# Linear attention and a butterfly feed-forward layer on one core: zeros for TensorE in the first pauses, a new order in the first and last slots, and all layer norms applied by VectorE

## The chip, the core and the metric

The kernel runs on one core of a Trainium2 chip. A core has a matrix engine (TensorE, PE in the rows; its weight loads are PEld), VectorE (DVE), ScalarE (ACT), GpSimd (POOL) and SyncE (SP), which here only issues DMAs. Each engine takes its own instructions in order and waits on semaphores for the others. The metric is the device time of one execution in microseconds (us), lower is better.

## The reference

One post-norm block on `x` of 4 x 1024 tokens with 128 features, in fp32:

```python
q, k, v = split(x @ W_qkv)                       # 16 heads of 64
q, k = relu(q @ W_f + b_f), relu(k @ W_f + b_f)  # per head
kv = einsum('bhnd,bhne->bhde', k, v)
out = einsum('bhnd,bhde->bhne', q, kv)
out = out / (einsum('bhnd,bhd->bhn', q, k.sum(2))[..., None] + 1e-6)
x1 = layernorm(x + out @ W_out + b_out)
h = butterfly(x1 @ W_exp + b_exp, up_weights)    # 512 features, 9 stages
h = butterfly(gelu(h + up_bias), down_weights)
y = layernorm(x1 + h @ W_con + b_con + down_bias)
```

## The kernel before

Weights are folded once on the chip: W_f into the key and query weights, the two butterflies into W_exp (by GpSimd, `up_step`) and W_con (by VectorE, nine steps `down_term`, `down_term`, `down_sum`, semaphore `s_dn`, three counts a step). Large fp32 products are split into a high and a low fp32r part, and three products make one (`split`, L671).

The tokens are 32 tiles of 128, and 8 chunks of 512. All engines walk through the same 43 slots (`SLOTS`), and each engine's code is a loop over the slots with its steps written out in order. Until slot 27 a slot holds: keys of a tile in two halves (`project_k`, taken by VectorE's `k_max`), the sum of keys times x (`add_kx`), two query steps (`project_q`, taken by ScalarE), two attention steps (`add_attn`, which need `qn`, its high part by ScalarE and its low part by VectorE's `qn_lo`), and, in some slots, up and down products of the feed-forward. The row names: `ring` is a ring of three PSUM banks that keys, queries, normalisers and up products share; `desk`, `spare_ps` and `attn_ps` are single banks; `kx_ps` holds the keys times x; `late` is the copied attention output; `hid` the hidden layer.

A use of the ring waits until the use three before it has been emptied. In a slot with a normaliser (every fourth) the order is key half 0, normaliser, query, key half 1, query, up product, so key half 1 waits for `k_max` of key half 0.

VectorE's order in a slot is: `k_max` of half 0, two `normalise_q`, then what the slot has of `reciprocal`, `m_lo`, `xT_lo`, `x1T_lo`, then `qn_lo`, `k_max` of half 1, `kx_end`, the residual sum with the statistics of a layer norm (`add_x` for norm 0, which makes x1, or `residual` for norm 1, which makes y), `qn_lo`. GpSimd raises the variance to the power -1/2 (`rstd_of`, L599). The norm is applied by ScalarE in the next slot (`layer_norm_apply`, L1134) before slot `APPLY_END` = 35, and by VectorE in the same slot, behind its last `qn_lo`, from there on (`layer_norm_end`, L1399).

The reciprocal of the normaliser goes to DRAM in four DMAs and comes back spread over partitions in eight (`spread`), on SP's queue, between the loads of butterfly coefficients, each of which waits for a step of the butterfly:

```python
load_down(5)
load_down(6)
spread(0)
load_down(7)
```

The first attention step (`add_attn(0)`, in slot 11) waits for `s_dn` at 3 * `PS_LAST` = 21, since steps 1 to `PS_LAST` - 1 of the butterfly keep their second term in `attn_ps`.

Of the kernel before, what the change touches and what calls it, by code (L numbers as in the profile page):

```python
# [5 lines left out]
def postln_linear_attention_butterfly_ffn_kernel(  # L6
# [102 lines left out]
    MAPS_SLOT = {}  # L109
    for b in range(BATCH):  # L110
        MAPS_SLOT[TILES * b + ATTN_AT - 2] = (b, 0)
        MAPS_SLOT[TILES * b + ATTN_AT - (0 if b else 1)] = (b, 1)
    XT_SLOT = {2: (1, 0), 3: (1, 1), 8: (2, 0), 11: (2, 1)}
    for b in range(3, BATCH):
        XT_SLOT[TILES * b - 6] = (b, 0)
        XT_SLOT[TILES * b - 5] = (b, 1)
    ATTN_LAST = [ATTN_AT + (PAIRS // 2) * (n + 1) - 1 for n in range(ALLCH)]
    ATT_T_SLOT = {ATTN_LAST[n] + 1: n for n in range(LAST)}
    X1T_SLOT = {ATTN_LAST[n] + 2: n for n in range(LAST)}
    UPS = {}  # L120
    DOWN_SLOT = {}
    Y_SLOT = {}
# [61 lines left out]
    for s in range(SLOTS):  # L184
        order = []
        if s in ATT_T_SLOT:
            order.append(("attn", ATT_T_SLOT[s]))
        if s in KXT_SLOT:
            order.append(("kxT", *KXT_SLOT[s]))
        if s in MAPS_SLOT:  # L190
            order.append(("maps", *MAPS_SLOT[s]))
        if s == BIAS_T_SLOT:
            order.append(("bias",))
        if s in XT_SLOT and s <= max(DOWN_STEP_SLOT):
            order.append(("x", *XT_SLOT[s]))
        if s == FIRST:
            order.append(("vo", 3))
        if s in X1T_SLOT:
            order.append(("x1", X1T_SLOT[s]))
        for use in order:  # L200
            desk_of[use] = len(desk_of)
# [19 lines left out]
    with ctx:  # L221
        def sb(name, shape, dt=fp32):
            return ctx.enter_context(nc.sbuf_tensor(name, shape, dt))
# [213 lines left out]
        def _(sp):  # L437
# [57 lines left out]
            column(bout_col[:, :], b_out)  # L495
            for i in range(HT):
                column(bup_raw[:, i:i + 1], up_bias[i * 128:(i + 1) * 128])
            def spread(n):

                sp.wait_ge(s_r, n + 1)  # L500
                for j in range(4):
                    sp.dma_start(recip_rows[n, :, j * QT:(j + 1) * QT], recip[32 * j:32 * j + 2 * PAIRS, :])\
                        .then_inc(s_rst, 16)
                sp.wait_ge(s_rst, 64 * (n + 1))
# [24 lines left out]
            load_down(3)  # L529
            load_down(4)  # L530
            load_down(5)
            load_down(6)
            spread(0)
            load_down(7)
            load_down(8)
            for n in range(1, LAST + 4):
                if n >= 4:

                    store_out(n - 4)
                if n < ALLCH:  # L540
                    spread(n)
# [12 lines left out]
        def _(pool):  # L554
# [75 lines left out]
            for s in range(SLOTS):  # L630
                if s == WEIGHTS_SLOT:
                    pool.wait_ge(s_wuh, 1)
                    g.tensor_tensor(wup_l[:, :], y_up[:, :], wup_h[:, :].bitcast(fp32), ALU.subtract).then_inc(s_wul, 1)
                if s == WEIGHTS_SLOT:
                    pool.wait_ge(s_rows, 48)
                    g.tensor_tensor(bdn_row, bdn_row, bcon_row, ALU.add).then_inc(s_brow, 1)
                if s in ATT_T_SLOT:
                    rstd_of(0, ATT_T_SLOT[s])
                if s in Y_SLOT:
                    rstd_of(1, Y_SLOT[s])  # L640
                if s in X1T_SLOT:
                    with_bias(X1T_SLOT[s], slice(0, QUADS), X1T_SLOT[s] + 1)
# [23 lines left out]
        def _(pe):  # L666
# [228 lines left out]
            def transpose_first_x(part):  # L895
# [2 lines left out]
                    last = t_.transpose(kx_ps[part][:, i * 128:(i + 1) * 128], xs[0][:, 2 * part + i, 0:C], ident[:, :])  # L898
                last.then_inc(s_xp, 1)

            pe.wait_ge(s_const, 2)
            transpose_first_x(0)
            pe.wait_ge(s_wk[0], 16)
            transpose_weights(PAIRS, 2, ring[0]).then_inc(s_wT, 1)
            transpose_first_x(1)
            pe.wait_ge(s_wf, 32)
            pe.wait_ge(s_wTd, 1)
            fold_wf(PAIRS, 2, attn_ps)

            for s in range(SLOTS):  # L910
                for kt in k_tiles(s)[:1]:
# [130 lines left out]
                down_group(LAST - 1, i, spare_ps[:, i * 128:(i + 1) * 128]).then_inc(s_dgrp, 1)  # L1042


            transpose_x1_half(0)
            take_down(LAST - 1)
            down_before_last(0)
            transpose_x1_half(1)
            down_before_last(1)
            up_half(0)  # L1050
            down_before_last(2)
            down_before_last(3)
# [9 lines left out]
        def _(act):  # L1062
# [89 lines left out]

            act.wait_ge(s_xp, 1)
            hi(xT_h[:, 0, 0:256], kx_ps[0][:, 0:256], s_x01h)
            act.wait_ge(s_xp, 2)
            hi(xT_h[:, 0, 256:CH], kx_ps[1][:, 0:256], s_xTh)
            act.wait_ge(s_fold, 1)
            hi(wk_h[:, 0:256], attn_ps[:, 0:256], s_wh)
            act.wait_ge(s_bf, 16)
            a_.activation(bf_minus[:, :], bf_row[:, :], ACT.Copy, scale=-1.0).then_inc(s_bfm, 1)  # L1160

            for s in range(SLOTS):
# [98 lines left out]
        def _(dve):  # L1261
# [177 lines left out]
            lo(xT_l[:, 0, 0:256], kx_ps[0][:, 0:256], xT_h[:, 0, 0:256], s_x01l)  # L1439
            dve.wait_ge(s_xTh, 1)  # L1440
            lo(xT_l[:, 0, 256:CH], kx_ps[1][:, 0:256], xT_h[:, 0, 256:CH], s_xTl)
            dve.wait_ge(s_wh, 1)
            lo(wk_l[:, 0:256], attn_ps[:, 0:256], wk_h[:, 0:256], s_wl)

            def w_lo(n, dst, high):
                dve.wait_ge(s_wh, n)
# [2 lines left out]
            for s in range(SLOTS):  # L1449
# [23 lines left out]
                for kt in k_tiles(s)[:1]:  # L1473
                    k_max(kt, 1)
                if s == 0:
                    w_lo(2, wk_l[:, 256:CH], wk_h[:, 256:CH])
                if s == 1:
                    w_lo(3, wk_l[:, CH:2 * CH], wk_h[:, CH:2 * CH])
                if s == 2:
# [2 lines left out]
                for kt in k_tiles(s)[1:]:  # L1482
                    k_max(kt, 0)
                if s == 0:
                    v.reduce_sum(x_part[:, 0, 1:2], desk[:, :], axis=mybir.AxisListType.X).then_inc(s_dtaken, 1)
                    v.reduce_sum(x_part[:, 0, 0:1], kx_both[:, :].rearrange("p (a n) -> p a n", a=2)[:, :, 0:256],
                                 axis=mybir.AxisListType.XY).then_inc(s_xpart, 1)
                if s == 1:
                    w_lo(4, wq_l[:, 0:CH], wq_h[:, 0:CH])
                for kt in k_tiles(s)[1:]:  # L1490
                    k_max(kt, 1)
                if s == 3:
                    down_term(0, 1)
                if s in KXT_SLOT:
# [55 lines left out]
                layer_norm_half(0, g, attn_ps[:, g * HALF:(g + 1) * HALF], xs[(BATCH - 1) % XBUF][:, at:at + 2, 0:C],  # L1550
                                last_x1[:, tiles, :], (s_x1sum, g + 1))
            layer_norm_half_end(0, 0, last_x1, s_x1)
            layer_norm_end(1, LAST - 2, y[:, (LAST - 2) % 2, :, :], s_yo)
            layer_norm_half_end(0, 1, last_x1, s_x1)
            for g in range(2):
                tok = slice(g * HALF, (g + 1) * HALF)
                use = ("x1", LAST, g)
                dve.wait_ge(s_x1h, LAST + 1 + g)
                lo(x1T_l[:, tok], half_bank(use)[:, 0:HALF], x1T_h[:, tok], half_taken(use)[0])
# [35 lines left out]
```

## Time and profile before

| | |
|---|---|
| median of 3 runs | 324.87 us (323.04 to 325.10) |
| profiled execution | 323.96 us, its rows span 322.1 us |
| TensorE busy | 302.8 us, 94% |
| VectorE busy | 218.7 us, 68% |
| ScalarE busy | 142.6 us, 44% |
| GpSimd busy | 96.0 us, 30% |
| mean granted clock of TensorE | 0.996 |

The profiled execution lies 1.86 us above its span and 0.91 us below the median. Times in rows are counted from the start of the span.

### The profile page before, as it was taken

What the parts mean: (1) busy time and instruction counts of PE and PEld (TensorE: products, weight loads), DVE (VectorE), ACT (ScalarE), POOL (GpSimd) and SP (SyncE); (2) the same over time, 40 slices, a digit from 0 to 9 for tenths busy, and PEclk for the clock granted to TensorE, in tenths of its full rate; (3) what the DMA queues carried; (4) which work ended last, traced back from release to release, by engine and by line L of the source; (5) the groups of instructions that cost most, each with busy time, mean ns of one, the idle gap of its engine ahead of it and who ended that gap; (6) DMA issues with size and microseconds to landing.
All of it is one profiled execution on the core that took longest, in us unless ns stands there. A gap on an engine that the chain in (4) does not pass through costs nothing.

```text
span 322.1 us, 6555 instructions
## 1 busy us (share of the span) xinstructions
PE 302.8 (94%) x2521; PEld 268.2 (83%) x2521; DVE 218.7 (68%) x492; ACT 142.6 (44%) x267; POOL 96.0 (30%) x105
## 2 busy tenths in 40 slices
PE   4799999999699999999999999999999799999893
PEld 2799999988598898988899989998887587759793
DVE  4535568887898978658763794269548953768844
ACT  3223133324333454554562467256657846340452
POOL 3048998992000002400210121003203402513413
PEclk9999999999999999999999999999999999999998
DMA  5993493224922900640074005600190182462001
GB/s 133 288 335 106 126 263 136 113 86 140 240 85 75 211 5 7 163 101 0 4 171 94 2 36 121 146 0 35 38 225 5 40 200 62 117 159 55 1 35 65
DMA packets 23046, 34.02 MB, mean 106 GB/s; under 512 B 4040, under 2 KB 11112, under 8 KB 23016
## 3 DMA queue, kind: packets, MB, share of 16 engines
q1 hardware_dynamic: 22712, 33.54, 39.8%
q8 instruction: 20, 0.33, 0.4%
q10 hardware_dynamic: 304, 0.07, 0.1%
q14 instruction: 10, 0.08, 0.1%
HBM read 31.24 MB, written 2.36 MB: 104 GB/s over the span
## 4 chain that ended last, share of the span: by engine, by line
PE 79%; DVE 8%; issue 5%; DMA 3%; ACT 2%; SPq 1%; POOL 1%; POOLq 0%; DVEq 0%; ACTq 0%
PE ring L671 30%; PE kx_ps L770 16%; PE attn_ps L671 9%; PE spare_ps L871 8%; PE ring L788 4%; PE desk L680 3%; PE desk L802 2%; DMA recips<-recip_rows 1%; PE attn_ps L709 1%; DVE qn L1375 1%; PE attn_ps L822 1%; DVE stats L1384 1%; DMA xs<-in_L_attn_x_dram 1%; DMA recip_rows<-recip 1%; PE attn_ps L828 1%
## 5 line engine op out<-in xcount | busy, mean ns | idle before, releaser
L1327 DVE TENSOR_TENSOR k<-ring,bf_minus 128x512 f32<-128x512 f32 x64 | 43.9, 687 | 46.6 <-PE ring L671 46.5
L599 POOL TENSOR_TENSOR rstd<-var_eps,minus_half 128x4 f32<-128x4 f32 x14 | 19.3, 1380 | 164.8 <-DVE var_eps L1390 164.8
L1079 ACT ACTIVATE q<-ring,bf_col 128x512 f32<-128x512 f32 x64 | 43.7, 684 | 53.1 <-PE ring L671 52.9
L770 PE MATMUL kx_ps<-xs,k 128*128 128x129 f32 x512 | 62.4, 275 | 1.6 <-issue 1.6
L770 PEld LDWEIGHTS kx_ps<-xs,k 128*128 128x128 f32 x512 | 61.1, 191 | 3.4 <-issue 1.8
L1375 DVE TENSOR_TENSOR qn<-q,recips 128x512 f32<-128x512 f32 x64 | 43.3, 716 | 3.3 <-DMA recips<-recip_rows 3.3
L1071 ACT ACTIVATE qn_h<-qn 128x512 fp32r<-128x512 f32 x48 | 29.6, 627 | 26.8 <-DVE qn L1375 26.8
L671 PE MATMUL ring<-wk_h,xT_h 128*128 128x256 f32 x128 | 39.3, 307 | 1.0 <-DVE wk_l L1265 1.0
L1265 DVE TENSOR_TENSOR qn_l<-qn,qn_h 128x512 fp32r<-128x512 f32 x48 | 33.8, 712 | 7.7 <-ACT qn_h L1071 7.0
L671 PE MATMUL ring<-wk_l,xT_h 128*128 128x256 f32 x128 | 36.4, 284 | 0.0
L671 PE MATMUL ring<-wk_h,xT_l 128*128 128x256 f32 x128 | 36.4, 284 | 0.0
L582 POOL TENSOR_TENSOR y<-hid,y_up 128x512 f32<-128x512 f32 x18 | 27.6, 1557 | 18.5 <-DMA hid<-in_L_ffn_up_weights_dram 17.6
L1143 ACT ACTIVATE hid<-ring,bup_col 128x512 f32<-128x512 f32 x28 | 19.2, 687 | 22.9 <-PE ring L671 22.7
L671 PE MATMUL ring<-xT_h,wq_h 128*128 128x512 f32 x64 | 27.7, 434 | 0.0
L671 PEld LDWEIGHTS ring<-wk_h,xT_h 128*128 128x128 f32 x128 | 24.8, 193 | 3.3 <-issue 1.6
L871 PEld LDWEIGHTS spare_ps<-wdn,hid 128*128 128x128 f32 x224 | 25.9, 192 | 1.0 <-issue 0.8
L871 PE MATMUL spare_ps<-wdn,hid 128*128 128x128 f32 x224 | 26.7, 276 | 0.0
L671 PEld LDWEIGHTS ring<-wk_l,xT_h 128*128 128x128 f32 x128 | 24.9, 194 | 1.6
L671 PE MATMUL ring<-xT_h,wq_l 128*128 128x512 f32 x64 | 25.3, 395 | 0.0
L671 PE MATMUL ring<-xT_l,wq_h 128*128 128x512 f32 x64 | 25.2, 393 | 0.0
L671 PEld LDWEIGHTS ring<-wk_h,xT_l 128*128 128x128 f32 x128 | 24.7, 193 | 0.0
L671 PE MATMUL attn_ps<-qn_h,m_h 128*128 128x512 f32 x48 | 19.6, 407 | 3.1 <-issue 2.6
(158 smaller groups left out, 526.4 us busy)
## 6 DMA issues: line engine op xcount, KB each, us to landing
recips<-recip_rows SPq DMA_DIRECT2D x64, 256.0 KB, 5.5
hid<-in_L_ffn_up_weights_dram SPq DMA_DIRECT2D x9, 512.0 KB, 4.7
x<-_L_ffn_down_weights_dram SPq DMA_DIRECT2D x9, 512.0 KB, 3.9
xs<-in_L_attn_x_dram SPq DMA_DIRECT2D x7, 256.0 KB, 5.5
out_dram<-y SPq DMA_DIRECT2D x7, 256.0 KB, 2.1
q<-in_L_attn_W_qkv_dram SPq DMA_DIRECT2D x2, 512.0 KB, 5.5
q<-in_L_attn_W_out_dram SPq DMA_DIRECT2D x2, 256.0 KB, 7.7
recip_rows<-recip SPq DMA_DIRECT2D x32, 8.0 KB, 1.4
```

Of the source, the lines that this page charges most:

```text
L582: g.tensor_tensor(term_up[f].rearrange("p (hi j lo) -> p hi j lo", j=2, lo=lo), w[:, :, :, :, f], yv[:, :, f:f + 1, :].to_broadcast([128, ...
L599: g.tensor_tensor(rstd[i][:, :], var_eps[i][:, :], minus_half[:, :].to_broadcast([128, QUADS]), ALU.pow).then_inc(s_rs[i], 1)
L671: last = t_.matmul(dst, lhsT, rhs, start=start and n == 0, stop=stop and n == len(pairs) - 1)
L770: last = t_.matmul(kx_ps[g % 2][:, j * C1:(j + 1) * C1], k[kt % KRING][:, col:col + 128], xs[b % XBUF][:, QUADS * c + 2 * half + i, :], st ...
L788: last = t_.matmul(dst[32 * j:32 * j + 32, 0:QT], ksum_cols[:, p, :], q[:, (PAIRS * n + p) % QRING, j * QT:(j + 1) * QT], start=p == 0, st ...
L871: last = t_.matmul(dst, hid[:, j, i * 128:(i + 1) * 128], wdn[:, j, :], start=j == 0, stop=j == HT - 1)
L1071: a_.activation(dst, src, ACT.Copy).then_inc(done, 1)
L1079: a_.activation(q[:, i % QRING, :], bank(("q", i))[:, :], ACT.Relu, bias=bf_col[:, :])\
L1143: a_.activation(hid[:, i, :], bank(("up", f))[:, :], ACT.Gelu, bias=bup_col[:, i:i + 1])\
L1265: v.tensor_tensor(dst, src, high.bitcast(fp32), ALU.subtract).then_inc(done, 1)
L1327: v.tensor_tensor(k[kt % KRING][:, half * CH:(half + 1) * CH].rearrange("p (h d) -> p h d", d=D), bank(("k", kt, half))[:, :].rearrange("p ...
L1375: v.tensor_tensor(qn[:, a % NRING, :], q[:, a % QRING, :], recips[:, a % PAIRS // RC, a % RC, :], ALU.mult).then_inc(s_qn, 1)
```

## The change

Seven edits that stand apart:

- VectorE clears a tile `zeros` first of all, and TensorE multiplies it by itself 20 times before its first work, 6 times before the first fold of W_f, and 4 times before the first keys. The results go to `desk` and are not read.
- The first fold is put ahead of the transposes of the second half of the first x, with its followers on ScalarE and VectorE. In slot 0 VectorE makes `x_part` of `kx_ps`, for which `add_kx(0)` waits, earlier.
- `PS_LAST` is 6.
- The store of the reciprocal is split from `spread`, and for chunk 0 it stands ahead of `load_down(6)`.
- The second half of `head_maps` stands one slot earlier for all batches but the first.
- `APPLY_END` is 0: nine layer norms, five of x1 and four of y, leave ScalarE; the `mean_minus` and `offset` that ScalarE's form needs go with them. The transposes of x1 of chunk 4 go from the end of slot 32 to slot 33, behind its two query steps.
- At the end, TensorE's first down group of chunk 6 stands ahead of the transposes of the last x1, and VectorE applies both halves of the last x1 before the norm of y of chunk 5.

```diff
-        MAPS_SLOT[TILES * b + ATTN_AT - (0 if b else 1)] = (b, 1)
+        MAPS_SLOT[TILES * b + ATTN_AT - 1] = (b, 1)
...
-    X1T_SLOT = {ATTN_LAST[n] + 2: n for n in range(LAST)}
+    X1T_HEAD = {ATTN_LAST[4] + 3: 4}
+    X1T_SLOT = {ATTN_LAST[n] + 2: n for n in range(LAST) if n not in X1T_HEAD.values()}
...
-    APPLY_END = 35
+    APPLY_END = 0
...
-    PS_LAST = 7
+    PS_LAST = 6
...
             load_down(5)
+            store_recip(0)
             load_down(6)
             spread(0)
...
+            def multiply_zeros(n):
+                for _ in range(n):
+                    t_.matmul(desk[:, 0:128], zeros[:, :], zeros[:, :], start=True, stop=True)
+
+            pe.wait_ge(s_zeros, 1)
+            multiply_zeros(20)
             pe.wait_ge(s_const, 2)
             transpose_first_x(0)
             pe.wait_ge(s_wk[0], 16)
             transpose_weights(PAIRS, 2, ring[0]).then_inc(s_wT, 1)
-            transpose_first_x(1)
+            multiply_zeros(6)
             pe.wait_ge(s_wf, 32)
             pe.wait_ge(s_wTd, 1)
             fold_wf(PAIRS, 2, attn_ps)
+            transpose_first_x(1)
+            multiply_zeros(4)
...
-            transpose_x1_half(0)
             take_down(LAST - 1)
             down_before_last(0)
+            transpose_x1_half(0)
+            down_before_last(1)
             transpose_x1_half(1)
-            down_before_last(1)
...
                 if s == 0:
-                    w_lo(2, wk_l[:, 256:CH], wk_h[:, 256:CH])
+                    v.reduce_sum(x_part[:, 0, 0:1], kx_both[:, :].rearrange("p (a n) -> p a n", a=2)[:, :, 0:256],
+                                 axis=mybir.AxisListType.XY).then_inc(s_xpart, 1)
...
             layer_norm_half_end(0, 0, last_x1, s_x1)
-            layer_norm_end(1, LAST - 2, y[:, (LAST - 2) % 2, :, :], s_yo)
             layer_norm_half_end(0, 1, last_x1, s_x1)
             for g in range(2):
+                if g:
+                    layer_norm_end(1, LAST - 2, y[:, (LAST - 2) % 2, :, :], s_yo)
```

TensorE's first instructions, before (`kx_ps<-ident,xs` are transposes of x, `ring<-ident,q` of key weights, `attn_ps<-wf_diag,q` is the fold, `ring<-wk_h,xT_h` the first key product):

```order
L898 MATMUL kx_ps<-ident,xs 128x128 x2
L702 MATMUL ring<-ident,q 128x128 x2
L898 MATMUL kx_ps<-ident,xs 128x128 x2
L709 MATMUL attn_ps<-wf_diag,q 128x128 x2
L671 MATMUL ring<-wk_h,xT_h 128x256
```

And in the changed kernel, at the same place of TensorE's program:

```order
L916 MATMUL desk<-zeros 128x128 x20
L910 MATMUL kx_ps<-ident,xs 128x128 x2
L714 MATMUL ring<-ident,q 128x128 x2
L916 MATMUL desk<-zeros 128x128 x6
L721 MATMUL attn_ps<-wf_diag,q 128x128 x2
L910 MATMUL kx_ps<-ident,xs 128x128 x2
L916 MATMUL desk<-zeros 128x128 x4
L683 MATMUL ring<-wk_h,xT_h 128x256
```

The fold has moved ahead of the second transposes of x, and thirty products of zeros stand in between.

VectorE from the residual of slot 22 to the attention operands of slot 23, before (`y<-spare_ps,y` is `residual`, `k<-ring` is `k_max`, `qn_l` is `qn_lo`, `qn<-q,recips` is `normalise_q`):

```order
L1419 TENSOR_TENSOR y<-spare_ps,y 128x512
L1384 BN_STATS stats<-y 128x6 x4
L1386 MEMSET scratch 128x1
L1388 BN_AGGR mean_var<-stats 128x2 x4
L1390 TENSOR_SCALAR var_eps<-mean_var 128x4
L1393 TENSOR_SCALAR mean_minus<-mean_var 128x4
L1265 TENSOR_TENSOR qn_l<-qn,qn_h 128x512
L1327 TENSOR_TENSOR k<-ring,bf_minus 128x512
L1375 TENSOR_TENSOR qn<-q,recips 128x512 x2
L1265 TENSOR_TENSOR qn_l<-qn,qn_h 128x512
```

The same stretch of VectorE in the changed kernel:

```order
L1444 TENSOR_TENSOR y<-spare_ps,y 128x512
L1409 BN_STATS stats<-y 128x6 x4
L1411 MEMSET scratch 128x1
L1413 BN_AGGR mean_var<-stats 128x2 x4
L1415 TENSOR_SCALAR var_eps<-mean_var 128x4
L1290 TENSOR_TENSOR qn_l<-qn,qn_h 128x512
L1424 TENSOR_SCALAR y<-y,mean_var,rstd 128x128 x4
L1352 TENSOR_TENSOR k<-ring,bf_minus 128x512
L1400 TENSOR_TENSOR qn<-q,recips 128x512 x2
L1290 TENSOR_TENSOR qn_l<-qn,qn_h 128x512
```

Four instructions that apply the norm now stand between `qn_lo` and the next slot's `k_max`, and `mean_minus` is gone.

TensorE from the last up product of slot 32 to the first attention product of slot 33, before (`ring<-x1T...` is an up product, `desk<-ident,x` transposes x1 of chunk 4, `ring<-xT...,wq` are queries):

```order
L671 MATMUL ring<-x1T_h,wup_l 128x512
L680 MATMUL desk<-ident,x 128x128 x4
L671 MATMUL ring<-xT_h,wq_h 128x512
L671 MATMUL ring<-xT_l,wq_h 128x512
L671 MATMUL ring<-xT_h,wq_l 128x512
```

And in the changed kernel:

```order
L683 MATMUL ring<-xT_l,wq_h 128x512
L683 MATMUL ring<-xT_h,wq_l 128x512
L692 MATMUL desk<-ident,x 128x128 x4
L683 MATMUL attn_ps<-qn_h,m_h 128x512
L683 MATMUL attn_ps<-qn_l,m_h 128x512
```

The transposes have moved behind both query steps and stand directly ahead of the attention steps of slot 33.

## Rows read from the trace of the kernel before

**Rows 1.** Busy time per stretch: length, PE, PEld, DVE, ACT, POOL, clock, DMA share, GB/s.

```profile
16.00:66.00 50.00, 50.00 (x401) 48.48 (x402) 32.45 (x43) 14.91 (x28) 42.11 (x33) 1.00 0.57 178
89.00:246.00 157.00, 156.83 (x1330) 139.54 (x1329) 109.44 (x242) 81.54 (x152) 19.10 (x18) 1.00 0.33 77
```

**Rows 2.** Timeline of the start: start, busy time, engine, line, [idle before <-releaser].

```profile
1.23 1.76 DVE L1435 MEMSET q<- 128x2048 f32 x1 [1.23 <-PEq L1584]
...
3.27 0.66 PE L898 MATMUL kx_ps<-ident,xs 128*128 128x128 f32 x2 [3.27 <-POOL head_mask L569]
...
7.53 0.55 PE L671 MATMUL ring<-wk_h,xT_h 128*128 128x256 f32 x1 [1.02 <-DVE wk_l L1265]
...
8.31 0.41 PE L671 MATMUL ring<-wk_h,xT_h 128*128 128x256 f32 x1
...
8.53 0.41 PE L671 MATMUL ring<-wk_l,xT_h 128*128 128x256 f32 x1
...
12.27 0.28 PE L671 MATMUL ring<-wk_h,xT_h 128*128 128x256 f32 x1
...
12.39 0.28 PE L671 MATMUL ring<-wk_l,xT_h 128*128 128x256 f32 x1
...
15.22 0.68 DVE L1486 TENSOR_REDUCE x_part<-kx_ps 128x1 f32<-128x512 f32 x1
...
16.00 2.02 PE L770 MATMUL kx_ps<-xs,k 128*128 128x129 f32 x16 [1.63 <-issue]
```

**Rows 3.** Timeline of slots 8 to 11, DVE, SP's queue and PE.

```profile
68.80 0.95 DVE L1359 RECIPROCAL recip<-recip 128x128 f32<-128x128 f32 x1 [1.48 <-ACT recip L1117]
...
72.65 1.82 SPq L502 DMA_DIRECT2D recip_rows<-recip  x4
...
81.89 1.29 DVE L1375 TENSOR_TENSOR qn<-q,recips 128x512 f32<-128x512 f32 x2 [1.66 <-DMA recips<-recip_rows]
...
83.84 1.09 PE L802 MATMUL desk<-vo,kx 128*64 128x128 f32 x16 [0.44 <-DVE m_l L1265]
...
87.67 0.70 DVE L1294 TENSOR_TENSOR spare_ps<-late,attn_ps 128x512 f32<-128x512 f32 x1
...
88.47 0.47 PE L671 MATMUL attn_ps<-qn_h,m_h 128*128 128x512 f32 x1 [2.63 <-issue]
```

**Rows 4.** Timeline, slots 22 to 24, and VectorE's apply in a later slot.

```profile
183.57 1.46 POOL L599 TENSOR_TENSOR rstd<-var_eps,minus_half 128x4 f32<-128x4 f32 x1 [19.55 <-DVE var_eps L1390]
...
184.07 0.68 DVE L1327 TENSOR_TENSOR k<-ring,bf_minus 128x512 f32<-128x512 f32 x1
...
190.05 0.69 DVE L1327 TENSOR_TENSOR k<-ring,bf_minus 128x512 f32<-128x512 f32 x1
...
193.12 0.28 PE L671 MATMUL ring<-wk_h,xT_h 128*128 128x256 f32 x1
...
277.65 1.12 DVE L1399 TENSOR_SCALAR x<-x,mean_var,rstd 128x128 f32<-128x128 f32 x4 [0.90 <-POOL rstd L599]
```

**Rows 5.** Timeline, slots 31 to 33.

```profile
248.11 1.18 POOL L647 TENSOR_TENSOR xs<-xs,rows 128x512 f32<-128x512 f32 x1
...
248.19 1.65 DVE L1265 TENSOR_TENSOR qn_l<-qn,qn_h 128x512 fp32r<-128x512 f32 x1
...
251.95 0.69 DVE L1265 TENSOR_TENSOR qn_l<-qn,qn_h 128x512 fp32r<-128x512 f32 x1
...
252.78 0.47 PE L671 MATMUL attn_ps<-qn_h,m_h 128*128 128x512 f32 x1
...
256.19 0.63 PE L680 MATMUL desk<-ident,x 128*128 128x128 f32 x4 [1.76 <-ACT x L1134]
...
258.05 0.40 PE L671 MATMUL attn_ps<-qn_h,m_h 128*128 128x512 f32 x1
```

**Rows 6.** Timeline of PE, slot 35 and the end.

```profile
274.68 1.09 PE L802 MATMUL desk<-vo,kx 128*64 128x128 f32 x16 [0.47 <-DVE x L1408]
...
305.64 0.41 PE L1026 MATMUL desk<-ident,x 128*128 128x128 f32 x2 [1.08 <-DVE x L1539]
```

More of the change, by code:

```diff
@@ L187, in postln_linear_attention_butterfly_ffn_kernel @@
             order.append(("attn", ATT_T_SLOT[s]))
+        if s in X1T_HEAD:
+            order.append(("x1", X1T_HEAD[s]))
         if s in KXT_SLOT:
@@ L253, in postln_linear_attention_butterfly_ffn_kernel @@
         warm = sb("warm", [128, 1])
+        zeros = sb("zeros", [128, 128], fp32r)
         minus_half = sb("minus_half", [128, 1])
@@ L344, in postln_linear_attention_butterfly_ffn_kernel @@
         s_zero = sem("zeroed")
+        s_zeros = sem("zeros_for_tensor_made")
         s_wfz = sem("wf_zeroed")
@@ L497, in _, with store_recip @@
                 column(bup_raw[:, i:i + 1], up_bias[i * 128:(i + 1) * 128])
-            def spread(n):
+            def store_recip(n):
                 sp.wait_ge(s_r, n + 1)
@@ L503, in spread @@
                         .then_inc(s_rst, 16)
+            def spread(n):
                 sp.wait_ge(s_rst, 64 * (n + 1))
@@ L540, in _ @@
                 if n < ALLCH:
+                    store_recip(n)
                     spread(n)
@@ L640, in _ @@
                     rstd_of(1, Y_SLOT[s])
-                if s in X1T_SLOT:
-                    with_bias(X1T_SLOT[s], slice(0, QUADS), X1T_SLOT[s] + 1)
+                for at in (X1T_SLOT, X1T_HEAD):
+                    if s in at:
+                        with_bias(at[s], slice(0, QUADS), at[s] + 1)
                 if s == NO_KEYS + 2:
@@ L920, in _ @@
                         project_q(i)
+                if s in X1T_HEAD:
+                    transpose_x1(X1T_HEAD[s])
                 for a in adds(s)[:1]:
@@ L1154, in _ @@
             hi(xT_h[:, 0, 0:256], kx_ps[0][:, 0:256], s_x01h)
+            act.wait_ge(s_fold, 1)
+            hi(wk_h[:, 0:256], attn_ps[:, 0:256], s_wh)
             act.wait_ge(s_xp, 2)
             hi(xT_h[:, 0, 256:CH], kx_ps[1][:, 0:256], s_xTh)
-            act.wait_ge(s_fold, 1)
-            hi(wk_h[:, 0:256], attn_ps[:, 0:256], s_wh)
             act.wait_ge(s_bf, 16)
@@ L1169, in _ @@
                         q_relu(i)
+                if s in X1T_HEAD:
+                    x1T_hi(X1T_HEAD[s])
                 if s in LATE_NORM_SLOT:
@@ L1433, in x1T_lo @@
                 lo(x1T_l[:, :], desk[:, :], x1T_h[:, :], s_dtaken)
+            v.memset(zeros[:, :].bitcast(fp32), 0.0).then_inc(s_zeros, 1)
             v.memset(wout_diag, 0.0).then_inc(s_zero, 1)
@@ L1439, in _ @@
             lo(xT_l[:, 0, 0:256], kx_ps[0][:, 0:256], xT_h[:, 0, 0:256], s_x01l)
+            dve.wait_ge(s_wh, 1)
+            lo(wk_l[:, 0:256], attn_ps[:, 0:256], wk_h[:, 0:256], s_wl)
             dve.wait_ge(s_xTh, 1)
             lo(xT_l[:, 0, 256:CH], kx_ps[1][:, 0:256], xT_h[:, 0, 256:CH], s_xTl)
-            dve.wait_ge(s_wh, 1)
-            lo(wk_l[:, 0:256], attn_ps[:, 0:256], wk_h[:, 0:256], s_wl)
             def w_lo(n, dst, high):
@@ L1468, in _ @@
                     x1T_lo(X1T_SLOT[s - 1])
+                if s in X1T_HEAD:
+                    x1T_lo(X1T_HEAD[s])
                 if s in DOWN_STEP_SLOT:
@@ L1484, in _ @@
                 if s == 0:
-                    v.reduce_sum(x_part[:, 0, 1:2], desk[:, :], axis=mybir.AxisListType.X).then_inc(s_dtaken, 1)
-                    v.reduce_sum(x_part[:, 0, 0:1], kx_both[:, :].rearrange("p (a n) -> p a n", a=2)[:, :, 0:256],
-                                 axis=mybir.AxisListType.XY).then_inc(s_xpart, 1)
+                    w_lo(2, wk_l[:, 256:CH], wk_h[:, 256:CH])
                 if s == 1:
@@ L1491, in _ @@
                     k_max(kt, 1)
+                if s == 0:
+                    v.reduce_sum(x_part[:, 0, 1:2], desk[:, :], axis=mybir.AxisListType.X).then_inc(s_dtaken, 1)
                 if s == 3:
```

## Prediction

> **What bounds the kernel now.** I read the busy time by stretch first, since the share over the whole span mixes stages. From 16 to 66 us and from 89 to 246 us TensorE is busy for 50.00 of 50.00 and 156.83 of 157.00 us at a granted clock of 1.00, while VectorE works for 32.45 and 109.44 us of them [rows 1]. In these two stretches nothing but less work for TensorE can help, and no edit takes real work from it. So a gain must come from where TensorE waits. I looked for those places in the timeline of TensorE: the start, up to 16.00 us [rows 2]; slots 8 to 11 [rows 3]; the end of slot 32, where it waits 1.76 us [rows 5]; slot 35, 0.47 us, and the last transposes of x1, 1.08 us [rows 6]. For the moves on VectorE I asked the reverse: which TensorE instruction needs the result that now comes later, and how long before it that result was there [rows 4, 5]. What is won at the start isn't eaten by a later wait that I could find, because TensorE has no idle time between 16 and 66 us on which a load could have been about to arrive late.
>
> **The start.** TensorE starts with two transposes at 3.27 us, after a wait for GpSimd's constants. Its first key product starts at 7.53, after 1.02 us of waiting for the low part of the folded key weights. Key products then follow each other 0.22 us apart (8.31 to 8.53), but 0.12 apart from 12.27 on (to 12.39), and `add_kx(0)` starts at 16.00 after 1.63 us of idle time, with `x_part` ready at 15.22 + 0.68 = 15.90 [rows 2]. The spacing falls by a factor of two, as it would between TensorE's levels of 1.2 and 2.4 GHz. The slower pace ends some 4.5 us after TensorE became continuously busy at 7.53.
>
> The zeros can begin when VectorE has cleared their tile: it starts its first MEMSET at 1.23 us [rows 2], and one of 128 columns instead of 2048 takes about 1.76 / 16 = 0.11, so at about 1.4. No row shows an fp32r product of 128 columns. By columns it is half of one of 256, 0.11 us at the slow pace; at worst it costs what an fp32 product of 129 columns does, 2.02 / 16 = 0.126 at the fast pace [rows 2], so 0.25 at the slow. Twenty take 2.2 to 5.0 us and end between 3.6 and 6.4, where the transposes stood at 3.27. I take 0.11, since the rows of the same type are nearer. The fold then stands ahead of the second transposes, and the weights' low part ahead of VectorE's second x; the keys start at about 6.85 instead of 7.53. If TensorE is at the fast pace by 7.5, as 4.5 us from about 1.4 and the gaps between let me expect, its work from 7.53 to 14.37 (16.00 less 1.63) takes 6.84 - 2.3 = 4.5 us instead, since the slow 4.6 us up to 12.1 halve; that ends at 11.4, and 0.3 later for a slow beginning. `x_part` of `kx_ps` moves ahead of a weight split and two `k_max`, so that the 1.63 us goes, but for the 0.3 that VectorE still needs. `add_kx(0)` then starts at 12.0: **-4.0 us**. If the pace doesn't rise sooner, only the fold (0.7) and the idle time (1.3) are won, -2.0; the other end is -4.5.
>
> The Trainium skill, "TensorE: Matmul & The Clock Gate", has a clock for TensorE that rises when it has been kept busy and falls back in pauses, which agrees with the halved spacing in rows 2. By it products of zeros count as work, and the start comes out at the -4.0; no run here shows that yet.
>
> **Slots 8 to 11.** The first attention product waits 2.63 us until 88.47, behind a sum of VectorE that begins at 87.67 and takes 0.70 [rows 3]. That is step 6 of the butterfly. With `PS_LAST` at 6 the count is reached by step 5, a slot earlier, and the 2.63 goes. The reciprocal is ready at 68.80 + 0.95 = 69.75, but its store is issued only at 72.65, behind a coefficient load that waits for the butterfly. VectorE later waits 1.66 us for the spread copy, ahead of the `qn` at 81.89, and the maps' low part keeps TensorE waiting 0.44 at 83.84 [rows 3]. With the store 2.9 us earlier the 1.66 should go, and with it most of the 0.44. I count 2.63 + 0.44 = 3.07 and **-3.1**. What is late next is VectorE itself: if it isn't done with `qn_l` when the count is there, only about half is won, -1.5. If its 1.66 also shortens a stall of the keys behind it, it is -3.4. `load_down(6)` now stands behind the store, but the wait for step 5 on the same queue ends later than the reciprocal, so it pays nothing.
>
> **The maps.** In batches 1 to 3 half of `head_maps` comes a slot sooner. In slots 18 and 26 it meets `desk` just after the transposes of the keys' sum, which VectorE has to empty; by my reading of the same pair of steps in slot 35 (0.47 us of waiting [rows 6]) I take 0.25 for each, **+0.5**, bounds 0 and 0.94. For the third batch, slot 35's own 0.47 and a restart of 0.1 go: **-0.6**.
>
> **Layer norms on VectorE.** Each of the nine costs VectorE its wait for GpSimd's power and four scalings. In the slot that does this already it waits 0.90 us and works 1.12 [rows 4], so about 2.0 us each, 18 in all. ScalarE is rid of as much, but TensorE never waits for ScalarE except for the 1.76 us of rows 5. VectorE is idle for 47.6 us between 89 and 246 (157.00 - 109.44 [rows 1]), which is the cover of most. It fails where two norms lie in succession and VectorE has no gaps: slots 22 and 23, whose neighbours have a normaliser. There the power of slot 22 is ready at 183.57 + 1.46 = 185.03, whereas `k_max` started at 184.07. In slot 24 `k_max` of half 0 ends at 190.05 + 0.69 = 190.74, and TensorE's key half 1, which needs its bank, starts at 193.12: cover 2.38 [rows 4]. Two norms bring 4.1 and 190.74 becomes 194.8, so TensorE waits **+1.7**, bounds 0 and 2.5. The pairs in slots 15/16, 19/20 and 26/27 have larger gaps on VectorE around them, and I cost them at nothing; without that cover each would cost the same 1.7.
>
> In slots 30 to 33 VectorE has no slack: its `qn_l` of 251.95 ends at 252.64, and the attention product that needs it starts at 252.78 [rows 5]. Here the norm of y delays the next attention step by up to 2.0, and the norm of x1 the one behind it, while the transposes of chunk 4 no longer wait 1.76 for ScalarE. I have the attention product of 258.05 at 258.4 to 259.4, so **+0.9**; the bounds are -1.9 (all hidden and the 1.76 won) and +1.9. One `qn_l` in this stretch takes 1.65 us instead of 0.69, while GpSimd adds at 248.11 for 1.18 [rows 5].
>
> The Trainium skill, "GPSIMD Engine Reference", says that GpSimd and VectorE share access to SBUF; the 1.65 beside 0.69 agrees with that. By it an apply that meets GpSimd's work is stretched by up to the same 0.96, and the term would be +1.9 rather than +0.9.
>
> **The end.** The 1.08 us before the last transposes of x1 [rows 6] is filled by a down group that stood behind them, and the second half of x1 no longer waits for y's norm: **-1.1**, bounds 0 and -1.5.
>
> **The sum.** -4.0 - 3.1 + 0.5 - 0.6 + 1.7 + 0.9 - 1.1 = -5.7. The profiled execution took 323.96, which gives 318.3; from the median of 324.87, 0.91 higher, it is 319.2. The runs lie between 323.04 and 325.10, with the profiled one in the middle, so I lean to it: **318.5 us**. About 1%, 3.2 us, is what a measurement of this kernel can tell from no change.
>
> **The rivals.**
> - All norms hidden. For it: VectorE's 47.6 idle us. Against it: the cover of 2.38 in rows 4. Without +1.7 and +0.9, and with part of the 1.76, the time is 314 to 316; by both ends of all gains 313.5. Chance 0.2.
> - The zeros don't bring the fast pace sooner, or the pauses between them lose it again. For it: three waits remain between the groups of zeros. Start -2.0, so 320.5. Chance 0.15.
> - VectorE is late at slots 8 to 11. For it: the wait for the copy is VectorE's own, and it works without a gap behind it. -1.5 instead of -3.1, so 320.1. Chance 0.1.
> - Slow zeros: 0.25 a product puts the first transposes 3.1 us later and the keys at about 11 us; the fast pace then gives back what this takes, and the start is worth 0. 322.5. Chance 0.06.
> - Slower than before: the norms reach TensorE in most slots, because VectorE's wait for GpSimd puts every later `k_max`, `qn` and `qn_l` of the slot behind it. The gains without norms are 8.3 us. At 2.0 a norm this turns the sign from five uncovered ones on; all nine give 324 - 8.3 + 18 = 334. For it: the order itself, in which nothing passes the waiting apply. Against it: TensorE's lead of 2.38. Chance 0.04.
>
> The forecast itself has 0.45. The range 313.5 to 322 leaves out the slower case and the outer ends of two terms at once. Faster by over 1% (below 321.6): the forecast, the first three rivals nearly whole: 0.85. Within 1%: slow zeros and the outer parts of two others, 0.11. Slower 0.04.
>
> **What the changed profile would show.** Right: key products 0.12 apart from 7.5 us on; `add_kx(0)` near 12; the first attention product with no 2.63 ahead of it and `store_recip` at 70; nine waits of VectorE for `rstd` of about 0.9, and TensorE idle in slot 24 for some 1.7; no 1.76 at the transposes of chunk 4; the last transposes without 1.08. Wrong: a TensorE gap that grows behind `k_max` in several slots, a first transpose after 4 us, or a load of weights that TensorE now waits for before 66 us, since everything there comes 4 us sooner.

## The result and the profile after

The changed kernel is slower: 329.45 us against 324.52 in the median, a ratio of 1.0142 with a 95% interval of 1.0091 to 1.0193. The prediction said 318.5 and, with a chance of 0.85, faster. The profiled execution took 330.15 us and spans 328.4, 6.3 more than before. The first line of its page and the shares of its chain of waits by engine:

```profile
PE 310.5 (95%) x2551; PEld 274.8 (84%) x2551; DVE 228.5 (70%) x520; ACT 129.3 (39%) x231; POOL 93.6 (29%) x96
...
PE 78%; DVE 9%; issue 6%; POOL 3%; ACT 2%; POOLq 0%; DVEq 0%; ACTq 0%
```

TensorE is busier by 7.7 us though its real work is the same: 6.6 us lie between the starts of the zeros and of what follows them, and in slot 27 products ran at half pace. GpSimd is now on the chain with 3%; those are the powers for which VectorE's norms wait.

Where the 6.3 us arise is best read by putting the starts of the same TensorE instructions side by side. The last column is what a stretch added or took.

| TensorE instruction | before | after | later by | stretch |
|---|---|---|---|---|
| first `add_kx(0)` | 16.00 | 15.70 | -0.30 | start -0.3 |
| first attention product, slot 11 | 88.47 | 84.85 | -3.62 | slots 8 to 11 -3.3 |
| last attention step of slot 18 | 141.71 | 138.00 | -3.71 | -0.1 |
| first attention step of slot 20 | 157.91 | 155.84 | -2.07 | slots 18, 19 +1.6 |
| last of slot 24 | 193.83 | 193.44 | -0.39 | slots 22 to 24 +1.7 |
| last of slot 26 | 212.43 | 212.04 | -0.39 | 0 |
| first of slot 28 | 228.56 | 233.43 | +4.87 | slots 26, 27 +5.3 |
| last of slot 33 | 258.74 | 265.15 | +6.41 | slots 29 to 33 +1.5 |
| end of the span | 322.1 | 328.4 | +6.3 | -0.1 |

Two stretches are far from the forecast: the start and slots 26 and 27. The start first, in the timeline of the changed kernel, against [rows 2]:

```profile
1.05 4.53 PE L916 MATMUL desk<-zeros 128*128 128x128 f32 x20 [1.05 <-DVE zeros L1460]
5.38 0.65 PE L910 MATMUL kx_ps<-ident,xs 128*128 128x128 f32 x2
...
9.61 0.55 PE L683 MATMUL ring<-wk_h,xT_h 128*128 128x256 f32 x1
...
10.39 0.41 PE L683 MATMUL ring<-wk_h,xT_h 128*128 128x256 f32 x1
10.60 0.41 PE L683 MATMUL ring<-wk_l,xT_h 128*128 128x256 f32 x1
...
12.01 0.28 PE L683 MATMUL ring<-wk_h,xT_h 128*128 128x256 f32 x1
12.13 0.28 PE L683 MATMUL ring<-wk_l,xT_h 128*128 128x256 f32 x1
...
15.70 1.95 PE L782 MATMUL kx_ps<-xs,k 128*128 128x129 f32 x16
```

Twenty products of zeros occupy TensorE from 1.05 to 5.38, 0.22 us each, as much as a key product of twice the columns. The first transposes come 2.1 us late, the keys start at 9.61 instead of 7.53, and at 10.39 they are still 0.21 apart; only from about 11.2 on are they 0.12 apart. The first transpose after 4 us is one of the signs of being wrong that the prediction named. The order of `x_part` does what was expected (TensorE doesn't wait just ahead of 15.70; 0.57 us of waiting for the low part of x are left at 13.32), and the two just cancel.

Slots 8 to 11, against [rows 3], VectorE, SP's queue and TensorE:

```profile
68.48 0.95 DVE L1384 RECIPROCAL recip<-recip 128x128 f32<-128x128 f32 x1 [1.41 <-ACT recip L1140]
...
69.46 1.73 SPq L508 DMA_DIRECT2D recip_rows<-recip  x4
...
79.83 1.28 DVE L1400 TENSOR_TENSOR qn<-q,recips 128x512 f32<-128x512 f32 x2
...
83.02 1.09 PE L814 MATMUL desk<-vo,kx 128*64 128x128 f32 x16
...
84.85 0.40 PE L683 MATMUL attn_ps<-qn_h,m_h 128*128 128x512 f32 x1
```

The store leaves as soon as the reciprocal is there, and the waits of 1.66, 0.44 and 2.63 are gone.

Now from the maps of slot 26 to the transposes of slot 27, the four engines in order of time:

```profile
217.10 0.60 ACT L1094 ACTIVATE m_h<-desk 128x512 fp32r<-128x512 f32 x1 [0.56 <-PE desk L814]
...
218.11 1.39 POOL L610 TENSOR_TENSOR rstd<-var_eps,minus_half 128x4 f32<-128x4 f32 x1 [24.77 <-DVE var_eps L1415]
...
219.54 1.12 DVE L1424 TENSOR_SCALAR y<-y,mean_var,rstd 128x128 f32<-128x128 f32 x4 [0.91 <-POOL rstd L610]
220.57 0.69 DVE L1352 TENSOR_TENSOR k<-ring,bf_minus 128x512 f32<-128x512 f32 x1
221.17 1.28 DVE L1400 TENSOR_TENSOR qn<-q,recips 128x512 f32<-128x512 f32 x2
222.37 0.69 DVE L1290 TENSOR_TENSOR m_l<-desk,m_h 128x512 fp32r<-128x512 f32 x1
...
223.11 1.11 PE L692 MATMUL desk<-ident,late 128*128 128x128 f32 x4 [3.08 <-DVE m_l L1290]
```

The maps of slot 26 fill the bank `desk`. Its next user is the transposition of the attention output in slot 27, and the bank is free only when VectorE has made `m_l` from it. ScalarE's half is ready at 217.70, but VectorE first finishes slot 26 with the norm of y, for which it waits 0.91 us, and then does `k_max` and two `qn` of slot 27. TensorE stands for 3.08 us. In the old order the maps stood behind that transposition, so that nobody asked for the bank so soon. What follows the pause is in the view of stretches (length, PE, PEld, DVE, ACT, POOL, clock, DMA share, GB/s):

```profile
219.60:223.10 3.50, 0.43 (x2) 0.00 (x0) 3.50 (x9) 1.21 (x3) 0.00 (x0) 0.99 0.19 75
223.10:226.50 3.40, 3.39 (x13) 3.19 (x14) 1.51 (x3) 0.51 (x1) 0.00 (x0) 0.51 0.02 5
226.50:230.00 3.50, 3.38 (x23) 2.73 (x21) 2.49 (x13) 0.77 (x2) 1.38 (x1) 1.00 0.00 0
```

Behind the pause the granted clock is 0.51 for 3.4 us, the 1.2 GHz level, which costs half of it, 1.7 us. That part doesn't come in every execution. In the profiled execution of no_zeros (the run without the products of zeros, see below) the same transposes wait as long, and the clock stays at 1.00:

```profile
220.87 0.66 PE L690 MATMUL desk<-ident,late 128*128 128x128 f32 x4 [3.07 <-DVE m_l L1279]
...
220.90:224.30 3.40, 3.40 (x27) 3.26 (x28) 2.52 (x7) 0.47 (x1) 0.00 (x0) 1.00 0.00 0
```

In the execution of the changed kernel slots 26 and 27 lose 3.1 + 1.7, and of the remaining 0.5 the maps themselves waited 0.3 in their new slot. In slot 19 the same wait is 1.21 us, without a norm ahead of `m_l` and without a fall of the clock.

The other two places, against [rows 4] and [rows 5]: slot 24, then slots 31 to 33.

```profile
190.85 1.12 DVE L1424 TENSOR_SCALAR x<-x,mean_var,rstd 128x128 f32<-128x128 f32 x4 [0.90 <-POOL rstd L610]
191.89 0.68 DVE L1352 TENSOR_TENSOR k<-ring,bf_minus 128x512 f32<-128x512 f32 x1
...
192.62 0.39 PE L683 MATMUL ring<-wk_h,xT_h 128*128 128x256 f32 x1 [0.90 <-DVE k L1352]
...
252.53 1.19 POOL L659 TENSOR_TENSOR xs<-xs,rows 128x512 f32<-128x512 f32 x1
...
252.59 1.99 DVE L1424 TENSOR_SCALAR y<-y,mean_var,rstd 128x128 f32<-128x128 f32 x4 [0.91 <-POOL rstd L610]
...
259.44 0.47 PE L683 MATMUL attn_ps<-qn_h,m_h 128*128 128x512 f32 x1 [0.69 <-DVE qn_l L1290]
...
262.29 0.60 PE L692 MATMUL desk<-ident,x 128*128 128x128 f32 x4
264.38 0.47 PE L683 MATMUL attn_ps<-qn_h,m_h 128*128 128x512 f32 x1 [1.49 <-DVE qn_l L1290]
```

Key half 1 of slot 24 waits for `k_max`, as forecast. The transposes of chunk 4 have lost their 1.76, but the attention products around them now wait for `qn_l`. One norm takes 1.99 us instead of 1.12 where it meets GpSimd's addition.

### The profile page after: what moved, and what is told of

Same layout as the page of the kernel before. It is cut to its first block, busy times and chain, and to the rows that moved or that the text cites. A ratio compares the mean times of both kernels' runs of the same rounds, so it can differ in the third digit from the quotient of the medians.

```text
span 328.4 us, 6589 instructions
## 1 busy us (share of the span) xinstructions
PE 310.5 (95%) x2551; PEld 274.8 (84%) x2551; DVE 228.5 (70%) x520; ACT 129.3 (39%) x231; POOL 93.6 (29%) x96
## 4 chain that ended last, share of the span: by engine, by line
PE 78%; DVE 9%; issue 6%; POOL 3%; ACT 2%; POOLq 0%; DVEq 0%; ACTq 0%
PE ring L683 27%; PE kx_ps L782 17%; PE attn_ps L683 8%; PE spare_ps L883 8%; PE ring L800 4%; PE desk L692 3%; POOL rstd L610 3%; PE attn_ps L834 2%; PE desk L814 2%; PE desk L916 2%; DVE qn L1400 2%; DVE stats L1409 1%; PE attn_ps L721 1%; ACT hid L1166 1%; DVE y L1444 1%
```

## The experiments

Two theories stood against each other for the loss behind slot 18. **The bank**: the earlier maps hold `desk` until `m_l`, and VectorE comes to `m_l` late. **The norms alone**: VectorE has too much to do, and where the maps stand is indifferent. For the start, either the zeros were too dear, or they did nothing for the pace, or both.

**maps_back**: the changed kernel with the old slot of the maps.

```diff
-        MAPS_SLOT[TILES * b + ATTN_AT - 1] = (b, 1)
+        MAPS_SLOT[TILES * b + ATTN_AT - (0 if b else 1)] = (b, 1)
```

> The changed kernel with the second half of the maps back in its old slot for batches 1 to 3, all else as changed. Theory one (the bank: the early maps hold the bank desk until VectorE's m_l, which stands behind k_max, two qn and in slot 27 a norm, so that TensorE's transposes of the attention output wait 1.21 and 3.08 us and TensorE runs 2.9 us at half pace after the second): both waits and the slow stretch go, some 5 of the 6.9 us lost there come back, 324 to 325 us. Rival (the norms alone: VectorE is late in these slots in any case, and the wait turns up at another TensorE instruction): at most 1 us comes back, 328.5 to 329.5 us.

Measured: 324.69 us, ratio 0.9995 (0.9966 to 1.0024), 4.8 less than the changed kernel. The bank theory holds. In the rows, slots 18 and 19 lose nothing more. But where the transposes of slot 27 no longer wait, the maps do:

```profile
222.38 1.09 PE L814 MATMUL desk<-vo,kx 128*64 128x128 f32 x16 [1.54 <-DVE x L1433]
```

VectorE is late with `add_x` by the norm of slot 26. This is the 1.6 us that remain there, with that norm as the cause and without a fall of the clock. Slots 22 to 24 (1.7) and 29 to 33 (1.5) lose as before.

**norms_back**: the changed kernel, early maps too, with the norms on ScalarE.

```diff
-    APPLY_END = 0
+    APPLY_END = 35
```

> The changed kernel with the norms before slot 35 on ScalarE again, all else as changed, the early maps too. The bank theory: the wait of the transposes stays at about 1.2 in slot 19 and falls from 3.08 to some 1.2 in slot 27, too short for the slow stretch; the 1.7 of slots 22 to 24 and the 1.5 of slots 30 to 33 go: 322 to 323.5 us. Rival (the norms alone): everything lost between slots 18 and 33 goes, about 10 us: 319 to 320 us.

Measured: 321.86 us, ratio 0.9924 (0.9894 to 0.9953). The transposes of slot 27 wait 1.20 us, as those of slot 19 did; by the starts slots 18 and 19 lose 1.6 and slots 26 and 27 1.9, and the only other place up to slot 32 that loses is the normaliser of slot 12, where TensorE waits 0.49 us for `k_max`. So the norms are not the whole; both edits cost time, and slot 27 is where they meet.

**m_first**: early maps and norms on VectorE stay, and only the place of `m_l` moves: for the second half of batches 1 and 2 it stands at the end of its own slot, ahead of the norm.

```diff
-                if s - 1 in MAPS_SLOT and STEPS * MAPS_SLOT[s - 1][0] < WHOLE:
+                if s - 1 in MAPS_SLOT and STEPS * MAPS_SLOT[s - 1][0] < WHOLE and MAPS_SLOT[s - 1] not in M_FIRST:
                     m_lo(*MAPS_SLOT[s - 1])
...
+                if MAPS_SLOT.get(s) in M_FIRST:
+                    m_lo(*MAPS_SLOT[s])
                 if s in ATT_T_SLOT and s >= APPLY_END:
```

> The changed kernel, early maps and all norms on VectorE kept, but VectorE makes m_l of the second half of the maps of batches 1 and 2 at the end of the same slot, ahead of the norm, instead of in the next slot behind k_max and two qn. The bank theory: both waits of the transposes (1.21 and 3.08) and the slow stretch behind the second go, though VectorE does the same work; 322.5 to 324.5 us. Rival (VectorE has too much to do there, with the norms, and which step is first doesn't matter): the wait turns up at the next key or attention product, 328 us or more.

Measured: 324.11 us, ratio 0.9974 (0.9948 to 0.9999), 5.3 less than the changed kernel with the same instructions. VectorE makes `m_l` where it waited for GpSimd, and the transposes start without a wait:

```profile
217.36 0.69 DVE L1291 TENSOR_TENSOR m_l<-desk,m_h 128x512 fp32r<-128x512 f32 x1
218.35 1.12 DVE L1425 TENSOR_SCALAR y<-y,mean_var,rstd 128x128 f32<-128x128 f32 x4 [0.31 <-POOL rstd L611]
...
218.68 0.60 PE L693 MATMUL desk<-ident,late 128*128 128x128 f32 x4
```

That settles the bank theory: the same work in another order takes the wait away.

**maps_alone**: the edit of the maps alone, in the kernel before.

```diff
-        MAPS_SLOT[TILES * b + ATTN_AT - (0 if b else 1)] = (b, 1)
+        MAPS_SLOT[TILES * b + ATTN_AT - 1] = (b, 1)
```

> The kernel before with the second half of the maps a slot earlier as the only edit; the norms stay on ScalarE. The bank theory: TensorE waits some 1.2 to 1.4 for m_l in slot 19 and again in slot 27, with no slow stretch: 3 us slower than before, 326.5 to 328 us. The prediction's term (0.25 in each of the two slots, 0.6 won in slot 35): within 0.5 of before.

Measured: 328.6 us, ratio 1.0119 (1.0066 to 1.0171), a little more than expected. By the starts of the attention steps it loses 1.64 in slots 18 and 19 and 1.87 in 26 and 27, 3.5 in sum; TensorE's transposes wait there for `m_l`, with the norms of these slots on ScalarE:

```profile
222.64 0.66 PE L680 MATMUL desk<-ident,late 128*128 128x128 f32 x4 [1.20 <-DVE m_l L1265]
```

**no_zeros**: the changed kernel without the products of zeros (and without their tile).

```diff
-            pe.wait_ge(s_zeros, 1)
-            multiply_zeros(20)
...
-            multiply_zeros(6)
...
-            multiply_zeros(4)
```

> The changed kernel without the thirty products of zeros, all else as changed. If they only cost time (0.22 us each, and the pace rises by what real work TensorE has done): first transposes at 3.3, keys at about 7, add_kx(0) at 14 to 14.5 instead of 15.7, 328 us. If they brought the fast pace sooner: keys start at about 7 but run at 0.22 until 12 or later, add_kx(0) at 15 to 15.7, 329 to 329.5 us.

**wide_zeros**: products of 256 columns, half as many.

```diff
-                    t_.matmul(desk[:, 0:128], zeros[:, :], zeros[:, :], start=True, stop=True)
+                    t_.matmul(desk[:, 0:256], zeros[:, 0:128], zeros[:, :], start=True, stop=True)
...
-            multiply_zeros(20)
+            multiply_zeros(10)
```

> The changed kernel with products of zeros of 256 columns instead of 128, half as many (10, 3 and 2). If a product of 128 columns costs as much as one of 256 (0.22 us at the slow pace), all zeros end 3.2 us sooner in sum, the keys start at 7 to 7.5 and add_kx(0) at 13 to 14: 327 to 328 us. If a product costs by its columns, 0.43 us each, nothing changes: add_kx(0) at 15.7, 329.5 us.

**narrow_half**: products of 128 columns, half as many (10, 3 and 2).

> The changed kernel with half as many products of zeros (10, 3 and 2) of 128 columns, which by the rows take as long as the products of 256 columns of wide_zeros. If TensorE's pace rises by the time that it has been occupied: as there, keys 0.12 apart from about 7 us, add_kx(0) at 12.2. If narrow products do less for the pace than wide ones: keys start at 7 but stay 0.22 apart until 9 to 11, add_kx(0) at 13 to 13.8, as without any zeros; 327 us.

Measured: no_zeros 327.04 us (ratio 1.0106, 1.0038 to 1.0174), wide_zeros 326.55 (1.0064, 1.0037 to 1.0091), narrow_half 328.09 (1.0073, 1.0041 to 1.0105). The times lie too close together for the three to be told apart; the rows tell more. First wide_zeros:

```profile
1.19 2.50 PE L916 MATMUL desk<-zeros 128*128 128x256 f32 x10 [1.19 <-DVE zeros L1460]
3.49 0.63 PE L910 MATMUL kx_ps<-ident,xs 128*128 128x128 f32 x2
...
7.31 0.28 PE L683 MATMUL ring<-wk_h,xT_l 128*128 128x256 f32 x1
7.42 0.28 PE L683 MATMUL ring<-wk_h,xT_h 128*128 128x256 f32 x1
...
12.22 1.95 PE L782 MATMUL kx_ps<-xs,k 128*128 128x129 f32 x16
```

Then narrow_half:

```profile
1.05 2.40 PE L916 MATMUL desk<-zeros 128*128 128x128 f32 x10 [1.05 <-DVE zeros L1460]
...
8.49 0.41 PE L683 MATMUL ring<-wk_h,xT_h 128*128 128x256 f32 x1
8.71 0.41 PE L683 MATMUL ring<-wk_l,xT_h 128*128 128x256 f32 x1
...
13.66 1.95 PE L782 MATMUL kx_ps<-xs,k 128*128 128x129 f32 x16
```

Ten products take 2.3 us with 256 columns and 2.2 with 128. Behind the wide ones the keys run 0.11 apart from the first on, and `add_kx(0)` starts at 12.22, where the forecast had it (12.0). Behind the narrow ones they are 0.21 apart until 9.1, and it starts at 13.66, about as in no_zeros, where the fast pace comes at about 11.2:

```profile
13.52 1.95 PE L780 MATMUL kx_ps<-xs,k 128*128 128x129 f32 x16
```

The new order of the start is thus worth some 2.5 us by itself, wide zeros another 1.3, and the thirty narrow ones take 2.2 away. These figures come from one execution each. With the old start `add_kx(0)` began at 15.50, 16.00 and 16.38 in three kernels (maps_alone, before, store_alone), so each is uncertain by some 0.5 us.

**store_alone**: the kernel before with two edits.

```diff
-    PS_LAST = 7
+    PS_LAST = 6
...
             load_down(5)
+            store_recip(0)
             load_down(6)
             spread(0)
```

> The kernel before with PS_LAST 6 and the early store of the first reciprocal as the only edits. By the prediction's term, which the changed kernel's trace bears out so far: 3.1 us less than before, 320.5 to 321.5 us. If the gain needs the shifted start of the changed kernel: 1.5 less, 322.7 us.

Measured: 320.9 us, ratio 0.9877 (0.9847 to 0.9907), 4.0 less than before in the median. By the starts, 3.3 of it are won between `add_kx(0)` (16.38) and the first attention product (85.58), as in the changed kernel. The term stands without the other edits; how it divides between `PS_LAST` and the early store was not tried.

**best**: maps_back, norms_back and wide_zeros in one; the other edits stay.

> The changed kernel with three edits mended: the maps in their old slot, the norms before slot 35 on ScalarE, and products of zeros of 256 columns, half as many. What stays: the new start, PS_LAST 6, the early store, the transposes of chunk 4 in slot 33 and the order of the end. If the terms read from the runs so far add up: -3.8 (start), -2.9 (slots 8 to 11), -1.4 (chunk 4) and -0.9 (end) give -9.0 from 324.2, 315 us, 314.3 to 316.5. If the norms leaving ScalarE was what the transposes of chunk 4 lived on, 316.5 to 317.5.

Measured: 315.37 us, ratio 0.9713 (0.9679 to 0.9746), faster than both kernels. Its starts are 3.9 ahead of the kernel before at `add_kx(0)`, 7.3 in slot 11 and still 7.35 at the end of slot 32, so that TensorE keeps all of it; 8.8 at the end.

**norms_on_best**: best with `APPLY_END` 0.

> The best version so far (315.4 us) with one edit undone: the nine norms are on VectorE again, the maps stay in their old slot. By the marks of maps_back, which loses 1.7 in slots 22 to 24, 1.6 in slots 27 and 28 and 2.3 in slots 30 to 35 and doesn't have the 1.4 won at chunk 4: 6 to 7 us more than best, 321 to 322.5. By the prediction's terms (1.7 and 0.9, with the maps at nothing): 318.

Measured: 321.63 us, ratio 0.9883 (0.9855 to 0.9911): the nine norms on VectorE cost 6.3 us where nothing else is wrong. By the starts, 1.7 in slots 22 to 24, 1.6 in 27 and 28, and 2.8 from slot 29 to 35 beside best; 0.5 lies at the start of this execution.

**norms_later**: the same nine norms on VectorE, up to slot 34 applied in the next slot behind `k_max` of half 1.

```diff
                 for kt in k_tiles(s)[:1]:
                     k_max(kt, 1)
+                if s <= APPLY_LATER + 1 and s - 1 in ATT_T_SLOT:
+                    n = ATT_T_SLOT[s - 1]
+                    layer_norm_end(0, n, x1[:, n % X1BUF, :, :], s_x1)
+                if s <= APPLY_LATER + 1 and s - 1 in Y_SLOT:
+                    n = Y_SLOT[s - 1]
+                    layer_norm_end(1, n, y[:, n % 2, :, :], s_yo)
```

> As norms_on_best, but VectorE applies each norm of slots up to 34 in the next slot, behind its k_max of half 1, when GpSimd's power has long been there. If the price is VectorE's wait for GpSimd (0.9 of the 2.0 us of each) and that it stands ahead of k_max, qn and m_l: most of the loss goes, 316 to 318 us. If the price is the 1.1 us of work in stretches where VectorE has no slack: 320 us or more, near norms_on_best.

Measured: 316.59 us, ratio 0.9728 (0.97 to 0.9755). VectorE does the same scalings, and 5.0 of the 6.3 us are back. The groups of its norms, first norms_on_best, then norms_later (busy, mean ns of one, idle before them):

```profile
L1424 DVE TENSOR_SCALAR x<-x,mean_var,rstd 128x128 f32<-128x128 f32 x28 | 7.8, 343 | 6.4 <-POOL rstd L610 6.4
L1424 DVE TENSOR_SCALAR y<-y,mean_var,rstd 128x128 f32<-128x128 f32 x24 | 7.6, 378 | 4.6 <-POOL rstd L610 4.6
```

```profile
L1425 DVE TENSOR_SCALAR x<-x,mean_var,rstd 128x128 f32<-128x128 f32 x28 | 7.8, 341 | 1.8 <-POOL rstd L611 1.8
L1425 DVE TENSOR_SCALAR y<-y,mean_var,rstd 128x128 f32<-128x128 f32 x24 | 6.7, 339 | 1.2 <-POOL rstd L611 1.2
```

8 us of waiting for GpSimd are gone, the work is nearly the same. In slots 22 to 24 nothing is lost. The price is the place of the norm, with its wait, ahead of what TensorE needs next, and only to some 1 us the work (1.2 us are left to best, 0.4 of them at the start of this execution). The place and the wait moved together, so that their shares are not shown apart.

**tail_back**: best with the old order of the end on both engines.

> The best version so far with the old order of the end on TensorE and VectorE. If the new order is worth what the marks show (0.9 to 1.1, the wait of 1.08 before the last transposes): 316.2 to 316.6 us. If the end is bound by what follows in any case: 315.4, as best.

Measured: 316.63 us, ratio 0.9732 (0.9699 to 0.9765), 1.3 above best, of which 0.5 lies already at the start of this execution. Between the last attention step and the end best wins 1.0, and tail_back nothing.

## Why the prediction was wrong, point by point

**The start** (-4.0; measured -0.3): wrong in the price of a product of zeros and in what it brings. I took 0.11 us by columns; it is 0.22, inside the bounds, and my preference for the row of the same type over the dearer one was the mistake. That dearer row, read by the starts (16 products from 16.00 to 17.86), gives 0.12 us at the fast pace and so 0.23 at the slow. At 0.22 the zeros end at 5.4 and not at 3.6. The second step, that the pace would be fast by 7.5, also failed for these products: it was so behind wide ones. The rival "slow zeros" described the outcome, a start worth 0, and had a chance of 0.06; but what makes up for the zeros here is mostly the new order, worth 2.5 us in no_zeros, where the rival had the fast pace do it. That the start came to -0.3 is partly luck: `add_kx(0)` lies between 14.88 and 15.96 in four executions with the same zeros. The Trainium skill, "TensorE: Matmul & The Clock Gate", Part 1, which I had cited as agreeing, lets the clock rise once TensorE has been kept busy; with products of 256 columns the trace agrees (0.11 apart at 7.31), with those of 128 it doesn't, since TensorE is occupied from 1.05 on and the keys are still 0.21 apart at 10.39.

**Slots 8 to 11** (-3.1; -3.3): right, and alone as well.

**The maps** (+0.5 with bounds 0 and 0.94, and -0.6 in slot 35; measured +1.6 and, with the norm of slot 26, +5.3): this is the step that turned the sign. Of the 5.3, 1.7 are the fall of the clock, which the same wait didn't bring in no_zeros. I looked at what the maps wait for in their new slot, `desk` emptied by VectorE, and found the 0.3 that is there. I did not look at who takes `desk` next, and what stands ahead of `m_l` on VectorE. Alone the edit costs 3.5 us. The 0.6 of slot 35 didn't come either: the maps of slot 34 wait in their turn, 0.69 us for the low part of x1.

**The norms** (+1.7 and +0.9; +1.7 and +1.5): 22 to 24 is right in place and size. Slots 30 to 33 lie within the bounds, between the forecast and the 1.9 that GpSimd's share was to bring: one norm took 1.99. The pair in 26 and 27 was costed at nothing and is uncovered: it costs 1.6 with the maps in their old slot (norms_on_best), as the prediction said it would without cover, and with the early maps it lengthens a wait of 1.2 to one of 3.1, behind which the clock fell in the profiled execution. Nine norms cost 6.3 where the forecast had 2.6.

**The end** (-1.1; -1.0): right.

**Sum.** Of the 12 us between forecast (-5.7) and measured (+6.3), 3.7 come from the start, 6.4 from slots 18, 19, 26 and 27 (1.7 of them the clock), 0.6 from slots 29 to 33, and 1.6 from slot 35 and the end together. The slower rival had another mechanism, five or more norms that each reach TensorE; it didn't happen that way. The nine norms alone cost 6.3, less than the 8.3 of gains, and norms_on_best, which has them all, is faster than the kernel before.

## What to carry to other kernels

When a step that fills a shared bank is moved earlier, ask who takes the bank next, and what the engine that empties it has queued ahead of the emptying; the wait appears there, not at the moved step. An operation with a wait on a slow helper belongs behind what the critical engine needs next: the same nine norms cost 6.3 us at the end of their slot and 1.2 one step into the next. Work that only warms an engine is priced by a row of the same shape, or tried alone, before it stands ahead of the first real work.

## What the runs showed of the hardware that was not expected

An fp32r product of 128 columns takes as long as one of 256 at the slow pace, 0.22 us (ten in 2.20 and 2.30 us). Each of these products has a weight load of 128 columns of its own, and these too follow each other every 0.22 us (twenty in 4.34), so whether the product or its load sets the time is not shown. Behind wide ones the keys were 0.11 to 0.12 apart from about 7 us on in five executions; in four executions with thirty narrow ones the spacing halved at about 9, 11 and 11 us and, in m_first, not before 13. `add_kx(0)` started at 14.88 to 15.96 in these and at 12.12 to 12.66 in five with wide ones. Why the turn varies among executions of the same start is open. Pauses of 3.07 to 3.08 us were followed by some 3.4 us at a granted clock of about 0.5 in three executions (the changed kernel, wide_zeros, narrow_half) and by none in a fourth (no_zeros); pauses of 1.20, 1.21, 1.54 and, in the kernel before, 2.63 us were not followed by a fall. What decides between them is open. In these first 16 us the granted clock reads 1.00 while products stand at twice their later distance, so there the spacing has to be read.
